# The last two attention iterations of a fused decoder layer as a program of their own

## The chip, the core and the metric
The kernel runs on one core of one Trainium2 chip. The metric is the device time of one execution in microseconds (us). Engines: TensorE (PE; its weight loads are PEld), VectorE (DVE), ScalarE (ACT), GpSimd (POOL), and SyncE (SP), which issues most DMAs.

## What is computed
A decoder layer over x of shape (8, 256, 256): 8 batches, 256 rows, width 256, all fp32.
```python
x = x + attn(layernorm(x))                    # softmax(exp(-|q - k|^2)) @ v, one head
x = x + cross(ctx, layernorm(x), mask)        # 16 heads of width 16, softmax(q k / 4)
x = x + ffn(layernorm(x))                     # 8 experts, best 2 of each row

logits = xs @ Wg                              # xs: 2048 rows
weights, sel = top_k(logits, 2); weights = softmax(weights)
h = relu(xs @ W1[e] + b1[e])                  # width 1024
out = sum over the 2 experts of weights * (h @ W2[e] + b2[e])
```

## The kernel before
**Stages.** Work on a batch is spread over iterations: in iteration n the stages of batch n (first attention's output, cross-attention's keys and queries), n-1 (maxima of the scores), n-2 (exponentials and weighted values) and n-3 (heads, output product, third norm, router) are issued in an interleaved order, which is written out by hand, per engine, in attention_tensor (L745), attention_scalar (L805), attention_vector (L850), attention_gpsimd (L917) and attention_sync (L939). Iterations run from -1 to 9. Iterations 8 and 9 have no new batch: 8 holds the maxima of batch 7, the exponentials of batch 6 and the output of batch 5; 9 holds the exponentials of batch 7 and the output of batch 6. They are called the drain here. The output of batch 7 is made inside the expert stage.

**Scores.** Queries and keys are split into a high and a low part and stacked over 48 partitions (q_stack, k_stack, three buffers each, by batch modulo 3). They are made twice. st_scores (L1382): 8 steps a batch; TensorE opens a pair of PSUM banks with four mask products (mask_product, L1339, the matmuls of L1346), adds the scores (L1376), and VectorE takes the maxima (L1388). st_maxima (L1393) then transposes the maxima (L1401), and SP writes them with four small DMAs into two more rows of q_stack (L1419). st_exps (L1451): again 8 steps; masks (L1346), products with 50 rows, so that the maximum is taken off (L1445), and ScalarE's exponential of 128 x 1024 (L1462). Which pair a step uses is told by scores_pair (L1350) and exps_pair (L1354): from batch 1 on the maxima have pair 1 and the exponentials pair 0; only batch 7's exponentials use both in turn. TensorE is issued both kinds as quad (L737). After every second exponential st_weighted (L1467, matmuls L1480) makes the weighted values of 4 heads; ScalarE copies them out after every fourth.

**Behind them.** st_heads_transposed (L1492, matmuls L1504), st_transpose "hT" (matmuls L1068), st_output (L1520, matmuls L1099), the third norm (VectorE and GpSimd, then L1021), st_router_transpose (L1550, matmuls L1557), st_router (L1566, matmuls L1572), st_best (L1733).

**Routing.** The rows' places in the experts' tiles are worked out with one-hot tables, in two parts: batches 0 to 4 in the drain, 5 to 7 in the expert stage. Part 0: routing_choice (L1744), prefix_product on TensorE (L1689), routing_counts (L1775), first_tiles (L1847), routing_slots (L1903) and four times routing_table (L1933): one-hot rows (L1948), values (L1953) and three products tile_vals (L1956), all on VectorE. TensorE multiplies each (table_product, L1701), b1_transpose (L1713) follows, and routing_index (L1961) makes the lists of rows. GpSimd then starts the gathers (ex_gather, L2144, the copy L2148 and the indirect DMA L2151).

**Expert stage.** experts (L2004) is a pipeline over 39 tiles of 128 rows: gather, transposes (L2177), first product (L2213), relu and split (L2223, L2230, L2233), second product (L2253), bias and weight (L2265, L2267), and an indirect DMA that adds to the output (L2166). W2 of an expert is loaded by SP (load_expert, L1617) and split into two parts in place, the high one by ScalarE (L1652), the low one by VectorE (L1657), 2048 elements wide; the second product of the first three tiles waits for the splits it needs, that of the fourth for all. The loads take the memory of buffers that the attention no longer needs, so SP waits for the last exponentials (t_tile) of batches 5, 6 and 7, for memory_over (L1581) and for the last transposes (p_hT) between them (experts_sync L1589, experts_rest_sync L1601). SP, like each engine, runs its list in order.

The diff's functions, with the line numbers of the profile:

## Time and profile before
| | us |
|---|---|
| median of 3 runs | 640.5 (638.93 to 642.87) |
| the profiled execution, device time | 644.66 |
| its span, first to last instruction | 642.9 |
| TensorE busy | 574.8 (89%) |
| VectorE busy | 360.0 (56%) |
| ScalarE busy | 331.2 (52%) |
| GpSimd busy | 220.1 (34%) |
| iteration 8, iteration 9, first expert tile | from about 278, 317, 358.7 |

Rows come from one profiled execution of the kernel. Busy times of TensorE are from its start to its modelled end; the granted clock is a share of 2.4 GHz, and 0.5 is the lower of its two levels, 1.2 GHz. A chain is followed back from the last instruction; "issue" is time in which an engine waited for nothing that the profile shows.

### The profile page before, as it was taken

The numbers are of one execution on the slowest core, as the hardware profiler recorded it, in microseconds if no ns is written. First come the engines' busy times: TensorE is split into PE (matmuls) and PEld (weight loads), VectorE is DVE, ScalarE is ACT, GpSimd is POOL, SyncE is SP. The second block draws the span as 40 slices with busy tenths as digits, with TensorE's granted clock in tenths as the row PEclk, the third lists the DMA queues.
The fourth block names the chain that finished last, engine by engine and source line by source line (L and its number), as shares of the span: only waits on it lengthen the run. The fifth ranks groups of instructions, "written<-read, shape, count | busy, mean of one in ns | idle before, by whom it ended". The sixth has DMA issues, their size and how long they took to land.

```text
span 642.9 us, 15591 instructions
## 1 busy us (share of the span) xinstructions
PE 574.8 (89%) x5107; PEld 491.4 (76%) x5108; DVE 360.0 (56%) x856; ACT 331.2 (52%) x723; POOL 220.1 (34%) x289
## 2 busy tenths in 40 slices
PE   4677899999999999865877799999999999999992
PEld 3575667787777777543444799999999999999991
DVE  3647776868686867646465867665233232333321
ACT  4532467555656465422343674555655656555560
POOL 6512212213132321000004514543454555555532
PEclk9978999999999999978567799999999999999996
DMA  8594443545445361720065956566667576676732
GB/s 224 134 154 77 52 82 37 93 60 81 70 65 87 54 98 25 111 67 29 9 198 188 316 203 171 167 173 202 201 177 221 176 213 195 191 216 174 224 94 24
DMA packets 56009, 85.71 MB, mean 133 GB/s; under 512 B 6673, under 2 KB 44721, under 8 KB 55953
## 3 DMA queue, kind: packets, MB, share of 16 engines
q1 hardware_dynamic: 46368, 73.59, 45.2%
q0 software_dynamic: 7872, 10.33, 8.5%
q10 hardware_dynamic: 1712, 1.05, 0.6%
q8 instruction: 34, 0.56, 0.4%
q14 instruction: 23, 0.18, 0.1%
HBM read 62.44 MB, written 9.31 MB: 112 GB/s over the span
## 4 chain that ended last, share of the span: by engine, by line
PE 45%; DMA 30%; DVE 7%; issue 7%; ACT 5%; SPq 3%; POOLq 1%; POOL 1%; DVEq 0%; ACTq 0%
DMA out<-y,scatter_now 26%; PE bank L1099 13%; PE pair L1346 5%; PE bank L1480 5%; PE pair L2213 4%; PE pair L1445 4%; PE bank L2253 3%; SPq L1419 3%; PE pair L1376 2%; PE bank L1068 2%; DMA q_stack<-max_lo 2%; DVE row_max L1388 2%; DMA exp_ring<-L_attn_Wo 1%; PE bank L1572 1%; DMA experts_w<-L_ffn_W 1%
## 5 line engine op out<-in xcount | busy, mean ns | idle before, releaser
L2213 PE MATMUL pair<-slots_t,w_now 128*128 128x128 f32 x1248 | 147.4, 277 | 0.0
L2213 PEld LDWEIGHTS pair<-slots_t,w_now 128*128 128x128 f32 x1248 | 144.1, 194 | 0.1
L2223 ACT ACTIVATE hid<-pair,b_tile 128x128 f32<-128x128 f32 x312 | 88.7, 367 | 54.8 <-PE pair L2213 53.3
L2233 DVE TENSOR_TENSOR hid_lo<-hid,hid_hi 128x1024 fp32r<-128x1024 f32 x39 | 47.8, 1225 | 108.0 <-ACT hid_hi L2230 98.3
L2166 POOL DMA_INDIRECT out<-y,scatter_now x39 | 64.7, 1658 | 114.4 <-DMA out<-y,scatter_now 79.9
L1462 ACT ACTIVATE exp_ring<-pair 128x1024 f32<-128x1024 f32 x64 | 65.7, 1028 | 59.6 <-PE pair L1445 58.5
L1388 DVE TENSOR_REDUCE row_max<-pair 128x4 f32<-128x1024 f32 x64 | 78.3, 1223 | 30.0 <-PE pair L1376 30.0
L2253 PE MATMUL bank<-experts_w,hid_hi 128*128 x624 | 82.7, 285 | 0.0
L2253 PEld LDWEIGHTS bank<-experts_w,hid_hi 128*128 128x128 f32 x624 | 75.8, 188 | 0.0
L2230 ACT ACTIVATE hid_hi<-hid 128x512 fp32r<-128x512 f32 x78 | 49.3, 632 | 4.7
L2151 POOL DMA_INDIRECT slots_in<-xn_rows,gather_now x39 | 41.2, 1055 | 25.8 <-POOL gather_now L2148 15.4
L1001 POOL TENSOR_SCALAR rstd<-moments 128x2 f32<-128x2 f32 x24 | 8.1, 340 | 120.1 <-DVE moments L998 120.0
L2148 POOL COPY gather_now<-gather_idx 128x1 uint32 x39 | 42.0, 1077 | 8.2 <-DVE jump L2000 8.2
L2253 PE MATMUL bank<-experts_w,hid_lo 128*128 x312 | 42.9, 279 | 0.0
L1480 PE MATMUL bank<-exp_ring,v_aug 128*32 128x256 f32 x512 | 39.9, 436 | 2.7 <-ACT exp_ring L1462 2.7
L2183 ACT ACTIVATE slots_t<-bank 128x256 f32<-128x256 f32 x39 | 14.9, 383 | 52.3 <-PE bank L2177 52.3
L2253 PEld LDWEIGHTS bank<-experts_w,hid_lo 128*128 128x128 f32 x312 | 39.1, 188 | 0.0
L1445 PEld LDWEIGHTS pair<-q_stack,k_stack 50*128 50x128 f32 x256 | 20.7, 200 | 23.8 <-issue 23.8
L1346 PE MATMUL pair<-mask_k,ident_bf 64*64 64x512 bf16 x128 | 27.2, 422 | 11.9 <-DMA q_stack<-max_lo 6.9
L1445 PE MATMUL pair<-q_stack,k_stack 50*128 50x256 f32 x256 | 34.6, 351 | 0.0
L1081 ACT ACTIVATE tr_hi<-bank 128x512 fp32r<-128x512 f32 x32 | 19.0, 595 | 26.5 <-PE bank L1068 26.5
L1346 PE MATMUL pair<-mask_q,ident_bf 64*64 64x512 bf16 x128 | 26.2, 406 | 6.5 <-DVE row_max L1388 6.2
(287 smaller groups left out, 1078.5 us busy)
## 6 DMA issues: line engine op xcount, KB each, us to landing
w_now<-L_ffn_W SPq DMA_DIRECT2D x39, 1024.0 KB
experts_w<-L_ffn_W SPq DMA_DIRECT2D x8, 1024.0 KB, 6.0
k_stack<-ck_hi SPq DMA_DIRECT2D x32, 128.0 KB, 4.1
q_stack<-cq_hi SPq DMA_DIRECT2D x32, 128.0 KB, 4.3
ctx_in<-ctx SPq DMA_DIRECT2D x8, 256.0 KB, 2.8
k_stack<-ck_lo SPq DMA_DIRECT2D x16, 128.0 KB, 5.3
q_stack<-cq_lo SPq DMA_DIRECT2D x16, 128.0 KB, 5.2
out<-x SPq DMA_DIRECT2D x7, 256.0 KB, 4.7
```

Source lines behind the costliest of these rows:

```text
L1099: mm = eng.matmul(out, a, b, start=start and i == 0, stop=stop and i == len(pairs) - 1, skip_group_check=True)
L1346: eng.matmul(pair[to, c * 512:(c + 1) * 512], core.ident_bf[left, left], part[left, :, :], start=True, stop=False, skip_group_check=True)
L1388: core.e["maxed"].at(eng.tensor_reduce(maxima, pair[:, :].rearrange("p (c t k) -> p c t k", c=KT, t=KT), AX.X, ALU.max))
L1445: mm = eng.matmul(pair[:, c * 512 + kt * S:c * 512 + (kt + 1) * S], k_stack[rows, i, kt * P:(kt + 1) * P], q_stack[rows, i, :], start=Fals ...
L1462: core.e["exp"].at(eng.activation(slots.rearrange("p c t q -> p (c t q)"), pair[:, :], ACT.Exp, scale=HD ** -0.5))
L1480: mm = eng.matmul(ps[32 * q:32 * q + 32, (g % 2) * S:(g % 2 + 1) * S], core.v_aug[b.p][:, kt, head, :], core.exp_ring[:, head % 8, kt, :], ...
L2166: core.rows_out.at(eng.indirect_dma_start(core.out_rows, bass.IndirectOffsetOnAxis(ap=core.scatter_now[b.p][:, :], axis=0), core.y[b.p][:, ...
L2213: mm = eng.matmul(banks[half][:, f * P:(f + 1) * P], core.w1_now[b.p][:, c, start:start + P], core.slots_t[b.p][:, c, :], start=c == 0, st ...
L2223: act = eng.activation(core.hid[:, g, :], banks[half][:, f * P:(f + 1) * P], ACT.Relu, bias=core.b1_tile[b.p][:, g:g + 1])
L2230: core.m["hid_hi"].at(eng.activation(core.hid_hi[b.p][:, part, :], core.hid[:, part, :], ACT.Copy))
L2233: core.m["hid_lo"].at(eng.tensor_tensor(core.hid_lo[b.p][:, :, :], core.hid[:, :, :], core.hid_hi[b.p][:, :, :].bitcast(F32), ALU.subtract))
L2253: mm = eng.matmul(ps[:, 0:D], left[b.p][:, f, :], core.experts_w[:, bass.ds(x * PLACE + (part * FT * D + f * D), D)], start=term == 0 and ...
```

## The change
1. The attention loop ends after iteration 7; the drain becomes a list of its own for each engine (drain_tensor and the others). TensorE makes all eight maxima steps of batch 7 first, then the eight exponentials of batch 6, then those of batch 7, each two steps at a time: open, open, products, products. Both pairs of banks serve the maxima of batch 7 and the exponentials of batches 6 and 7. The output of batch 5 lies among the maxima and the first exponentials, that of batch 6 among those of batch 7.
2. Routing part 0: the three copies behind the prefix product go to ScalarE (prefix_copies). routing_slots becomes routing_rows and routing_weights, and routing_table becomes routing_hot on VectorE and routing_values, which runs on GpSimd in part 0 (on VectorE as before in part 1). local_vals gets a second buffer. first_tiles moves behind the third table, routing_index behind the last low part of the drain. GpSimd's and VectorE's dependent instructions have a counter each (link, settle).
3. SP: load 2 starts at memory_over, not after the exponentials of batch 6; load 3 after those. ScalarE: split 1 comes among batch 7's maxima, splits 2 and 3 at the end. VectorE: split 1 moves from the drain into tile step 0 of the expert stage, the output and variance of batch 7 ahead of it, and everything of batch 7's norm moves from step 1 to step 0.
4. The stacks are placed anew: that of batch 5 alone, then 7, then 6. st_maxima of batch 7 uses bank 2 in place of bank 0.

```diff
             setup(core, eng)
-            for n in range(-1, NB + 2):
+            for n in range(-1, NB):
                 ATTENTION[name](core, eng, Step(n // 2, n % 2))
+            DRAIN[name](core, eng)
...
-    core.local_vals = [sb(f"local_vals{g}", [3, count(g), LOCAL[g]]) for g in range(2)]
+    core.local_vals = [[local_vals[0], sb("local_vals_odd", [3, count(0), LOCAL[0]])], [local_vals[1]]]
...
+def last_maxima(core, at, g):
+
+    for fn in (scores_open, scores_products):
+        for i in (2 * g, 2 * g + 1):
+            at(0, fn, i)
+
+def last_exps(core, at, back, g):
+
+    for fn in (exps_open, exps_products):
+        for i in (2 * g, 2 * g + 1):
+            at(back, fn, i)
+
+def drain_tensor(core, eng):
+    at = drain(core, "tensor", eng)
+    last_maxima(core, at, 0)
+    at(2, st_heads_transposed)
+    last_maxima(core, at, 1)
+    at(2, st_transpose, "hT")
+    last_maxima(core, at, 2)
+    prefix_product(core, eng, 0)
+    last_maxima(core, at, 3)
+    at(2, st_output)
+    at(0, st_maxima)
+    last_exps(core, at, 1, 0)
+    last_exps(core, at, 1, 1)
+    at(1, st_weighted, 0)
+    last_exps(core, at, 1, 2)
+    at(1, st_weighted, 1)
+    last_exps(core, at, 1, 3)
+    at(1, st_weighted, 2)
+    at(2, st_router_transpose)
+    last_exps(core, at, 0, 0)
+    at(1, st_weighted, 3)
+    at(2, st_router)
+    last_exps(core, at, 0, 1)
+    at(1, st_heads_transposed)
+    table_product(core, eng, 0, 0)
+    last_exps(core, at, 0, 2)
+    at(0, st_weighted, 0)
+    table_product(core, eng, 0, 1)
+    at(1, st_transpose, "hT")
+    last_exps(core, at, 0, 3)
+    at(0, st_weighted, 1)
+    at(1, st_output)
+    at(0, st_weighted, 2)
+    table_product(core, eng, 0, 2)
+    at(0, st_weighted, 3)
+    at(1, st_router_transpose)
+    at(1, st_router)
+    at(0, st_heads_transposed)
+    table_product(core, eng, 0, 3)
+    b1_transpose(core, eng)
+    at(0, st_transpose, "hT")
+
+def drain_scalar(core, eng):
+    at = drain(core, "scalar", eng)
+    at(2, st_transpose, "hT")
+    routing_exp(core, eng, 0)
+    prefix_copies(core, "scalar", eng, 0)
+    split_expert(core, "scalar", eng, 1)
+    at(0, st_maxima)
+    for i in range(6):
+        at(1, st_exps, i)
+    at(1, st_weighted, 1)
+    at(1, st_exps, 6)
+    at(1, st_exps, 7)
+    at(2, st_router_transpose)
+    at(0, st_exps, 0)
+    at(0, st_exps, 1)
+    at(1, st_weighted, 3)
+    for i in (2, 3, 4, 5):
+        at(0, st_exps, i)
+    at(1, st_transpose, "hT")
+    at(0, st_weighted, 1)
+    at(0, st_exps, 6)
+    at(0, st_exps, 7)
+    at(0, st_weighted, 3)
+    at(1, st_router_transpose)
+    split_expert(core, "scalar", eng, 2)
+    at(0, st_transpose, "hT")
+    split_expert(core, "scalar", eng, 3)
+
+def drain_vector(core, eng):
+    at = drain(core, "vector", eng)
+    at(0, st_scores, 0)
+    routing_choice(core, "vector", eng, 0)
+    at(0, st_scores, 1)
+    at(2, st_heads_transposed)
+    for i in range(2, 5):
+        at(0, st_scores, i)
+    at(2, st_transpose, "hT")
+    for i in range(5, 8):
+        at(0, st_scores, i)
+    at(0, st_maxima)
+    at(2, st_output)
+    at(2, st_moments, 2)
+    routing_counts(core, "vector", eng, 0)
+    routing_rows(core, "vector", eng, 0)
+    routing_weights(core, "vector", eng, 0)
+    routing_hot(core, "vector", eng, 0, 0)
+    at(2, st_normalise, 2)
+    routing_hot(core, "vector", eng, 0, 1)
+    at(2, st_router)
+    at(2, st_best)
+    at(1, st_heads_transposed)
+    routing_hot(core, "vector", eng, 0, 2)
+    at(1, st_transpose, "hT")
+    first_tiles(core, "vector", eng)
+    at(1, st_output)
+    at(1, st_moments, 2)
+    routing_hot(core, "vector", eng, 0, 3)
+    at(1, st_normalise, 2)
+    at(1, st_router)
+    at(0, st_heads_transposed)
+    at(0, st_transpose, "hT")
+    routing_index(core, "vector", eng, 0)
+    at(1, st_best)
+
+def drain_gpsimd(core, eng):
+    at = drain(core, "gpsimd", eng)
+    routing_numbers(core, "gpsimd", eng)
+    at(2, st_moments, 2)
+    for c in range(3):
+        routing_values(core, "gpsimd", eng, 0, c)
+    at(1, st_moments, 2)
+    routing_values(core, "gpsimd", eng, 0, 3)
+
+def drain_sync(core, eng):
+    at = drain(core, "sync", eng)
+    core.e["t_tile"].wait(eng, LAST_BATCH.back(2))
+    load_expert(core, eng, 1)
+    memory_over(core, eng)
+    load_expert(core, eng, 2)
+    at(0, st_maxima)
+    at(2, st_output)
+    at(2, st_normalise, 2)
+    experts_sync(core, eng)
+    core.e["t_tile"].wait(eng, LAST_BATCH.back(1))
+    load_expert(core, eng, 3)
+    eng.wait_ge(core.r["order"], 1)
+    eng.wait_ge(core.E["residual_early"], 16 * EARLY_BATCHES)
+    ex_load(core, "sync", eng, Step(0, 0))
+    at(1, st_output)
+    core.e["t_tile"].wait(eng, LAST_BATCH)
+    load_expert(core, eng, 7)
+    at(1, st_normalise, 2)
+    eng.wait_ge(core.r["table"], 4)
+    ex_load(core, "sync", eng, Step(0, 1))
+    core.e["p_hT"].wait(eng, LAST_BATCH)
+    load_expert(core, eng, 4)
+    for b in range(2):
+        core.rows_in.wait(eng, Step(0, b))
+    for x in (5, 6):
+        load_expert(core, eng, x)
+
...
 def scores_pair(core, b, i):
-    return core.pair[1 if b.v > 0 else i % 2]
+    return core.pair[i % 2 if b.v in (0, NB - 1) else 1]
 
 def exps_pair(core, b, i):
-    return core.pair[0 if b.v < NB - 1 else i % 2]
+    return core.pair[i % 2 if b.v >= NB - 2 else 0]
 
 def scores_open(core, name, eng, b, it, i):
     if i == 0:
         core.q_stacked.wait(eng, b)
         core.k_stacked.wait(eng, b)
-    if b.v == 0:
-        core.e["maxed"].wait(eng, b if i >= 2 else b.back(1), i - 2)
+    if b.v in (0, NB - 1):
+        if i >= 2:
+            core.e["maxed"].wait(eng, b, i - 2)
+        elif b.v > 0 and i == 0:
+            core.e["exp"].wait(eng, b.back(2))
+        elif b.v > 0:
+            core.e["maxed"].wait(eng, b.back(1))
     elif i == 0:
         core.e["maxed"].wait(eng, b.back(1))
     else:
...
 def st_maxima(core, name, eng, b, it):
-    ps = core.psum[0]
+    ps = core.psum[0 if b.v < NB - 1 else 2]
     if name == "tensor":
-        bank_free(eng, b, (core.e["ksq"], -2, 0), (core.e["cq_split"], -1, 1))
-        if b.v == NB - 1:
-            eng.wait_ge(core.r["counted"], 1)
+        bank_free(eng, b, (core.e["ksq"], -2, 0), (core.e["cq_split"], -1, 1), (core.e["hT_lo"], 2, 0))
         core.e["maxed"].wait(eng, b)
         for qt in range(KT):
             mm = eng.transpose(ps[0:H, qt * P:(qt + 1) * P], core.row_max[:, qt, :], core.ident[:, :])
...
-    if b.v == NB - 1 and i >= 2:
+    if b.v >= NB - 2 and i >= 2:
         core.e["exp"].wait(eng, b, i - 2)
-    elif b.v == NB - 1 and i == 1:
-        core.e["maxed"].wait(eng, b)
+    elif b.v == NB - 2:
+        core.e["maxed"].wait(eng, b.back(-1), 6 + i)
+    elif b.v == NB - 1:
+        core.e["exp"].wait(eng, b.back(1), 6 + i)
     elif i >= 1:
...
-        ps = core.psum[qt if b.v < NB - 1 else qt + 1]
+        ps = core.psum[qt if b.v < NB - 2 else qt + 1]
         if name == "tensor":
-            if b.v == NB - 1:
+            if b.v >= NB - 2:
                 core.e[("x2", "gate")[qt]].wait(eng, b.back(1))
...
+def prefix_copies(core, name, e, g):
+
+    r, n = core.r, PARTS[g].stop - PARTS[g].start
+    within, totals = (ap.rearrange("p (t e) -> p t e", e=NE) for ap in prefix_banks(core, g))
+    e.wait_ge(r["prefix"], g + 1)
+    for dst, src in ((core.totals, totals), (core.running[0], totals), (core.within, within)):
+        if name == "scalar":
+            e.activation(dst[:, 0:n, :], src, ACT.Copy).then_inc(r["counted"], 1)
+        else:
+            e.tensor_copy(dst[:, 0:n, :], src).then_inc(r["counted"], 1)
...
+def routing_hot(core, name, e, g, c):
 
     r, j, n, width = core.r, c // 2, count(g), LOCAL[g]
     first = PARTS[g].start + c % 2 * n
+    tiles, buf, bufs = slice(first, first + n), c % 2 if g == 0 else 0, 2 - g
+    row_hot, hot, vals = core.row_hot[g][buf], core.local_hot[g], core.local_vals[g][buf]
     if c >= 1:
+        e.wait_ge(r["hot"], 3 * (4 * g + c))
+    if c >= bufs:
+        e.wait_ge(r["slots"], 3 * (4 * g + c + 1 - bufs))
+        e.wait_ge(r["table"], 4 * g + c + 1 - bufs)
+    link(core, name, e.tensor_tensor(hot[:, :, :], bc(core.iota_f[:, 0:width], [P, n, width], 1),
+                                     bc(core.slot_tile[:, j, tiles], [P, n, width], 2), ALU.is_equal))
+    link(core, name, e.tensor_tensor(row_hot[:, :, :], bc(core.iota_f[:, :], [P, n, P], 1),
+                                     bc(core.slot_row[:, j, tiles], [P, n, P], 2), ALU.is_equal))
+    settle(core, name, e)
     for a, val in enumerate((core.token_f[:, tiles], core.weight_hi[:, j, tiles].bitcast(F32),
                              core.weight_lo[:, j, tiles])):
-        link(core, e.tensor_tensor(vals[:, a, :, :], hot[:, :, :], bc(val, [P, n, width], 2), ALU.mult))
-    settle(core, e)
+        e.tensor_tensor(vals[:, a, :, :], hot[:, :, :], bc(val, [P, n, width], 2), ALU.mult).then_inc(r["hot"], 1)
+
+def routing_values(core, name, e, g, c):
+
+    r, j, n, width = core.r, c // 2, count(g), LOCAL[g]
+    first = PARTS[g].start + c % 2 * n
+    tiles, buf, bufs = slice(first, first + n), c % 2 if g == 0 else 0, 2 - g
+    tile_vals, vals = core.tile_vals[g][buf], core.local_vals[g][buf]
+    e.wait_ge(r["hot"], 3 * (4 * g + c + 1))
+    if c >= bufs:
+        e.wait_ge(r["table"], 4 * g + c + 1 - bufs)
     for a in range(3):
-        last = e.tensor_tensor(tile_vals[:, :, a, :, :], bc(core.onehot[:, j, tiles, :], [P, n, NE, width], 3),
-                               bc(vals[:, a, :, :], [P, n, NE, width], 2), ALU.mult)
-    last.then_inc(r["slots"], 1)
-
-
...
-            for b in range(4):
+            for b in range(2):
+                ex_gather(core, name, eng, Step(b // 2, b % 2))
+            st_moments(core, name, eng, LAST_BATCH, it, 2)
+            for b in range(2, 4):
                 ex_gather(core, name, eng, Step(b // 2, b % 2))
         elif n in (2, 3):
             at(-2, ex_gather)
         elif n is None or n >= 6:
             at(0, ex_gather)
-        if n == 1:
-            st_moments(core, name, eng, LAST_BATCH, it, 2)
...
             split_expert(core, name, eng, 2)
         elif n == 1:
-            st_output(core, name, eng, LAST_BATCH, it)
-            st_moments(core, name, eng, LAST_BATCH, it, 2)
             split_expert(core, name, eng, 3)
-            st_normalise(core, name, eng, LAST_BATCH, it, 2)
             split_expert(core, name, eng, 7)
```

## Rows read from the trace of the kernel before
**Rows 1.** The page, part 2: granted TensorE clock in 40 slices of 16.07 us.
```profile
PEclk9978999999999999978567799999999999999996
```

**Rows 2.** Windows: stretch, length, busy us of PE, PEld, DVE, ACT, POOL; clock, DMA, GB/s.
```profile
278.00:317.00 39.00, 28.25 (x226) 16.22 (x226) 19.13 (x60) 10.21 (x13) 0.94 (x2) 0.67 0.13 41
317.00:355.00 38.00, 27.50 (x199) 16.80 (x197) 23.26 (x82) 14.70 (x16) 7.85 (x10) 0.68 0.56 179
355.00:383.00 28.00, 24.60 (x181) 23.53 (x180) 21.16 (x34) 21.73 (x42) 8.96 (x8) 0.86 0.79 255
...
500.00:600.00 100.00, 100.00 (x881) 100.00 (x880) 32.73 (x60) 58.68 (x168) 54.73 (x61) 1.00 0.67 197
```

**Rows 3.** The chain that ended last: start, us, what; where a DMA stands in it.
```profile
276.16 1.92 DMA q_stack<-max_lo
...
320.51 5.50 DMA experts_w<-L_ffn_W
```

**Rows 4.** The page, part 5: the two big readers of the score banks.
```profile
L1462 ACT ACTIVATE exp_ring<-pair 128x1024 f32<-128x1024 f32 x64 | 65.7, 1028 | 59.6 <-PE pair L1445 58.5
L1388 DVE TENSOR_REDUCE row_max<-pair 128x4 f32<-128x1024 f32 x64 | 78.3, 1223 | 30.0 <-PE pair L1376 30.0
```

**Rows 5.** The chain at the full clock: one double step, then weighted values.
```profile
253.44 0.56 PE pair L1346 x8
253.99 0.44 PE pair L1445 x4
254.43 0.24 PE pair L1376 x4
254.67 1.00 PE bank L1480 x16
```

**Rows 6.** The chain: the same at half clock, a hand-over, last exponential, last output product.
```profile
306.21 1.00 PE pair L1346 x5
307.21 0.73 PE pair L1445 x4
307.93 0.43 PE pair L1376 x4
308.36 1.86 PE bank L1480 x16
...
328.91 0.64 PE pair L1346 x4
329.55 0.73 PE pair L1445 x4
...
347.92 1.03 ACT exp_ring L1462
...
355.96 2.91 PE bank L1099 x12
```

**Rows 7.** Busy time of three short stretches, columns as in rows 2.
```profile
297.60:303.40 5.80, 0.03 (x4) 0.03 (x4) 5.32 (x31) 0.28 (x1) 0.00 (x0) 0.85 0.00 1
303.40:311.00 7.60, 7.60 (x52) 4.39 (x53) 3.01 (x4) 2.64 (x3) 0.00 (x0) 0.50 0.10 35
333.00:339.00 6.00, 6.00 (x61) 4.09 (x61) 5.75 (x19) 2.65 (x3) 1.18 (x2) 1.00 0.13 45
```

**Rows 8.** GpSimd's groups by shape, 120 to 270 us.
```profile
L1641 POOL TENSOR_TENSOR experts_w<-experts_w 128x256 fp32r<-128x256 f32 x8 | 5.9, 734 | 0.0
L1314 POOL TENSOR_TENSOR x<-x,bias_xattn_bo 128x512 f32<-128x512 f32 x4 | 5.2, 1295 | 21.2 <-DVE x L1308 21.2
```

**Rows 9.** The timeline, 320 to 368 us: start, us, engine, line, operation.
```profile
321.93 1.55 DVE L1956 TENSOR_TENSOR tile_vals<-onehot,local_vals 128x400 fp32r<-128x400 f32 x3
...
347.62 1.98 POOL L2148 COPY gather_now<-gather_idx 128x1 uint32 x1 [8.20 <-DVE jump L2000]
...
358.66 0.63 PE L2177 MATMUL bank<-ident,slots_in 128*128 128x128 f32 x2
```

**Rows 10.** The gathers' tile slots_in over the span: DMA time.
```profile
DMA to landing us min/median/max: 4.1/4.4/4.6
```

447 lines of the change are left out of this document (191 added, 256 removed).

## The prediction
> **What bounds the kernel now.** I read the windows by stage first, then the page's clock line, then the chain. From 500 to 600 us TensorE is busy for 100.00 of 100.00 us at the full clock (2.4 GHz) [rows 2]: the expert stage is bound by TensorE, and whatever is won before it moves its end by as much. The two drain iterations, 278 to 317 and 317 to 355 us, are different: TensorE is busy for 28.25 of 39 and 27.50 of 38 us, at a mean granted clock of 0.67 and 0.68 [rows 2], and these are the slices where the clock line falls to 5 to 8 tenths [rows 1]. So the 77 us hold 28.25 x 0.67 + 27.5 x 0.68 = 37.6 us of work at the full clock. The other 39 us are 21 us of idle time and some 18 us lost to half clock (1.2 GHz).
>
> The chain names the idle time. At 276.16 it stands on the DMA that puts the maxima into the stack, and from 320.51 on a 5.50 us DMA of expert weights [rows 3]: in both iterations the first exponential needs the maxima of the iteration just finished, and the second time ScalarE has an expert split, waiting for its load, ahead of it. From 297.6 to 303.4 TensorE does 0.03 us while VectorE does 31 small instructions (counts and tile tables) for 5.32 us [rows 7] ahead of a maximum. Maxima (1.22 us on VectorE) and exponentials (1.03 us on ScalarE) have one pair of banks each in iteration 8 [rows 4], so each can be made only after the last was read.
>
> **The change, part by part.** The times are those of the profiled execution: span 642.9 us, device time 644.66; the median of the runs is 640.5, 4.2 lower. I carry the difference over to the median.
>
> *Stage A: eight maxima of batch 7 alone.* VectorE sets it: 8 x 1.22 = 9.8 us of maxima [rows 4]. Between them stand the choice, batch 5's heads and its low part. VectorE's 19.13 us between 278 and 317 less 9.8 for maxima and 5.32 for the table block leave 4.0 [rows 2, 7]; about 3.2 of such work falls into stage A (an estimate). Steps now come in twos on two pairs: the opening of the second waits for the maximum just before, so VectorE waits for one mask and one product, 0.64 + 0.73 us at half clock [rows 6] and 0.1 for the signal, 1.5 us. Of four hand-overs the small work hides two. TensorE is too idle here to keep its clock, I assume, as between 303.4 and 311, where it is 0.50 after the hole ahead of it [rows 7]. VectorE can begin at about 276.2, as the chain leaves iteration 7 [rows 3]: 276.2 + 9.8 + 3.2 + 3.0 = 292.2. Batch 5's output product (2.91 us at half clock [rows 6]) lies beside the last two maxima but for about 1.0; the transposes of the maxima take 0.6 and the first exponential's mask and product 1.7. First exponential: 295.5 (now about 279). The DMA of the maxima is now hidden behind eight exponentials of batch 6.
>
> *Stage B: sixteen exponentials.* A group is two exponentials and one batch of weighted values. ScalarE needs 2 x 1.03 us [rows 4], and a hand-over stands between two groups (the second opening's masks and the signal 0.46, most of the 0.56 for two; a product 0.44 [rows 5]; together 0.90): 2.96 us at the full clock. TensorE needs 0.56 + 0.44 + 0.24 + 1.00 = 2.24 of these [rows 5]. At half clock it needs 1.00 + 0.73 + 0.43 + 1.86 = 4.02 [rows 6] and is itself the bound. The rest of TensorE's work is 37.6 - 12 x 1.24 - 8 x 1.00 = 14.7 us; about 3.2 of it lies in stage A, 11.5 in B.
> Full clock: 295.5 + 8 x 2.96 = 319.2; the rest fits mostly into the 0.7 us that each group leaves and beside ScalarE's copies, and I add 2 us for the router of batch 5, which waits for ScalarE. From the last exponential (start 347.92) to the end of the last transposes, 0.75 ahead of the output product at 355.96 [rows 6], it takes now 7.3 us with the exponential; I take 8 from its end, because batch 6's router stands in the queue too. End of the drain: 329.2 (now 355.2).
> Half clock: 295.5 + 8 x 4.02 + 2 x 11.5 = 350.7, and 3 for the last waits: 353.7.
> I take the full clock for three quarters: in B TensorE has 8 x 2.24 + 11.5 = 29.4 us of work for 34 us, 87%, and from 333 to 339, where it had work throughout, the clock was 1.00 [rows 7]; but the stretch 303.4 to 311 was as busy and stayed at 0.50 [rows 7], so B can begin low. 329.2 + 24.5 / 4 = 335.3.
>
> *Routing on GpSimd.* The three tile_vals products of each table, 1.55 us on VectorE [rows 9], go to GpSimd, 12 instructions of 400 elements. GpSimd takes 734 ns for 256 elements and 1295 for 512 [rows 8], so 1.05 us for 400 on that line: 3.1 a table. The trace has none with such broadcast patterns; bounds are 0.52 us (VectorE's) and 2.9 (each held up once like the copy of one column at 347.62, which took 1.98 us [rows 9], some 1.8 of them waiting). I take 1.05, nearest to rows 8; at 2.9 the last table would come 1.7 us too late (rival 3's sum). The tables begin when VectorE is through with maxima, output and counts, near 300, and are wanted by TensorE from 310 on, one per 3 to 6 us: hidden. VectorE loses 6.2 us of work, and the table block no longer stands ahead of a maximum; TensorE's 5.8 us hole goes.
>
> The Trainium skill (GPSIMD Engine Reference, section 8, Key points) says that GpSimd shares its SBUF interfaces with VectorE and contends with instructions that have two SBUF inputs. The trace agrees in one place: a 1-column copy took 1.98 us on GpSimd at 347.62 [rows 9]. By that rule the 12 products would be stretched by what VectorE does beside them, which is the upper bound above.
>
> *What is late next.* Now the index table is ready 8 us ahead of the last transposes and the gather is hidden. In the new order the index follows the last low part on VectorE. From the end of the transposes: 1.4 for high and low part, 1.2 for the index, 0.8 for GpSimd's copy and issue, 4.4 for the gather [rows 10] = 7.8 us to the first expert tile, against 358.66 - 355.2 = 3.5 now [rows 9]. That costs 4.3. First tile: 335.3 + 7.8 = 343.1.
>
> *Expert splits and loads.* ScalarE's splits 1 to 3 lie in waits of the drain; one VectorE split (2.3 us) moves behind the drain, beside which TensorE has the first hidden products and now idles for some 3.4 of 28 us [rows 2]: 0, with 2.3 as the other end. Loads of weights 4 to 6 still start from the last transposes and the first gathers, so they move with them. SP waits for the tile order (about 317) before it stores batch 6's output; nobody waits for that. Nothing after the first tile changes: TensorE is full, the end follows.
>
> Sum: 358.66 - 343.1 = 15.6 us. 644.66 - 15.6 = 629.1 in the profiled execution's terms, 640.5 - 15.6 = 624.9, said as 625, for the median.
>
> **The rivals.**
> 1. *The clock comes back early in B and stays:* drain ends at 329.2, first tile 337.0, gain 21.7: 619. For it: the output product of batch 5 is dense work right ahead of B. Against: hand-overs in every group.
> 2. *The clock stays at half:* drain ends at 353.7, first tile 361.5, 2.8 us later than now, less what a denser order loses less in the first expert tiles: 643, no change. For it: 303.4 to 311, 0.50 through 7.6 busy us [rows 7]. Against: 333 to 339. The Trainium skill (TensorE: Matmul & The Clock Gate, section "A second HAM failure mode: psum-queue depth-cycling") reports a kernel in which small idles between groups of matmuls, made by cycling through PSUM banks, let the clock swing between its levels; two pairs handed to and fro are such cycling. By it this rival would hold.
> 3. *Slower: GpSimd is the bound.* If a product with these patterns takes v us, the tables follow each other at 3v from 300.5, with the variance of batch 6 (1.5 us) in the queue, and what follows the last (table product, index, gather) takes 8: first tile at 310 + 12 v. It decides from 12 v > 33, v > 2.8, and is slower than now from v > 4.05. At v = 4.6, 365: 647. For it: broadcasts over four dimensions and contention [rows 9]. Against: the line of rows 8, a quarter of that.
> 4. *The gain is lost again in the first expert tiles*, because splits and loads are the bound there (ScalarE busy for 21.73 of 28 us [rows 2]): half of it stays, 633.
>
> **How the numbers follow.** Chances: forecast 0.48, rival 1 0.27, rival 2 0.12, rival 3 0.05, rival 4 0.08. About 1% (6.4 us) is what a measurement of this kernel can tell from no change. Faster by over 1% (below 634.1): forecast, rival 1 and most of rival 4, 0.82; same: 0.13; slower 0.05. The likeliest one's own range is 619 to 632 (share of full clock between a half and all). For 8 in 10 the range reaches below rival 1 (615 less estimates for the waits in B, 612) and into rival 2: 612 to 641.
>
> **What would show it.** Windows over the drain: first exponential of batch 6 near 295, eight maxima from 276 to 292; the last transposes near 335; no wait for the maxima's DMA ahead of an exponential; the PEclk line with fewer low slices. TensorE idle for some 4 us ahead of the first expert tile (L2177's counterpart near 343), released by the gather. GpSimd's products at about 1.05 us each. Wrong would be: exponentials paced at 4 us per group (clock), TensorE waiting for GpSimd at a table product, or the second expert tile waiting for splits. If the first tile comes 15 us earlier and the end does not, TensorE was not the bound after 400 us.

## The result, and the profile after

The changed kernel took 625.6 us (median of 4 runs, 621.4 to 626.0) against 640.2 us (4 runs, 638.9 to 642.9) beside it: ratio 0.974, 95% interval 0.971 to 0.977. A second time, together with the experiments, it was 626.5 against 640.9, ratio 0.975 (0.970 to 0.980). The forecast was 625. By the medians the gain is 14.5 us; the ratio, whose interval reaches just to the quotient of the two medians (0.977), puts it at some 16.5. The profiled executions have spans of 642.9 and 624.3 us, 18.6 apart; the one of before lay some 4 us above its median, as the prediction said, and the changed one lies on its own.

The clock line of the changed kernel's page, and from its list of groups the two of [rows 4]:
```profile
PEclk9969899999999999996996899999999999999997
L1512 DVE TENSOR_REDUCE row_max<-pair 128x4 f32<-128x1024 f32 x64 | 78.0, 1222 | 22.9 <-PE pair L1500 22.9
L1586 ACT ACTIVATE exp_ring<-pair 128x1024 f32<-128x1024 f32 x64 | 65.0, 1028 | 30.4 <-PE pair L1569 27.1 <-PE bank L1604 2.3
```
A maximum and an exponential take what they took. Over the whole span, ScalarE's idle time ahead of exponentials fell from 59.6 us to 30.4, and in place of a row of low slices [rows 1] stand two short dips with 9 between them.

Windows, columns as in [rows 2]: maxima, clock coming back, the exponentials, end of the drain, the wait for the gather, first expert tiles:
```profile
276.00:292.00 16.00, 11.92 (x82) 8.12 (x78) 12.00 (x18) 2.99 (x6) 1.33 (x7) 0.69 0.43 133
292.00:300.00 8.00, 6.61 (x66) 3.15 (x64) 6.63 (x35) 4.28 (x6) 0.94 (x2) 0.78 0.13 39
300.00:320.00 20.00, 19.03 (x228) 11.83 (x225) 12.29 (x51) 14.05 (x17) 7.78 (x9) 1.00 0.41 122
320.00:333.00 13.00, 8.29 (x51) 6.58 (x50) 5.92 (x17) 3.49 (x5) 4.23 (x5) 0.74 0.59 204
333.00:341.00 8.00, 3.59 (x14) 2.93 (x14) 5.99 (x18) 2.03 (x3) 4.88 (x7) 0.71 0.87 292
341.00:354.00 13.00, 10.94 (x74) 10.73 (x74) 11.09 (x10) 10.01 (x21) 11.77 (x9) 0.78 0.87 272
```
From 300 to 320 us TensorE is busy for 19.03 of 20 us at the full clock, where before it had 0.67 and 0.68 over the two iterations of the drain [rows 2]. Behind it come two waits, each with a lower clock.

The timeline, VectorE, ScalarE and TensorE (start, us, engine, line, operation, wait before it and who ended it):
```profile
276.01 1.23 DVE L1512 TENSOR_REDUCE row_max<-pair 128x4 f32<-128x1024 f32 x1 [0.31 <-PE pair L1500]
...
284.30 1.23 DVE L1512 TENSOR_REDUCE row_max<-pair 128x4 f32<-128x1024 f32 x1 [1.46 <-PE pair L1500]
...
288.71 2.36 DVE L1512 TENSOR_REDUCE row_max<-pair 128x4 f32<-128x1024 f32 x2 [1.46 <-PE pair L1500]
293.37 1.94 ACT L1586 ACTIVATE exp_ring<-pair 128x1024 f32<-128x1024 f32 x2 [0.62 <-PE pair L1569]
296.61 1.94 ACT L1586 ACTIVATE exp_ring<-pair 128x1024 f32<-128x1024 f32 x2 [1.30 <-PE pair L1569]
299.96 1.94 ACT L1586 ACTIVATE exp_ring<-pair 128x1024 f32<-128x1024 f32 x2 [1.42 <-PE pair L1569]
302.84 1.94 ACT L1586 ACTIVATE exp_ring<-pair 128x1024 f32<-128x1024 f32 x2 [0.45 <-PE pair L1569]
305.72 1.94 ACT L1586 ACTIVATE exp_ring<-pair 128x1024 f32<-128x1024 f32 x2 [0.45 <-PE pair L1569]
308.94 1.94 ACT L1586 ACTIVATE exp_ring<-pair 128x1024 f32<-128x1024 f32 x2 [0.78 <-PE pair L1569]
313.14 1.94 ACT L1586 ACTIVATE exp_ring<-pair 128x1024 f32<-128x1024 f32 x2 [2.27 <-PE bank L1604]
317.28 0.60 ACT L1612 ACTIVATE heads_t<-bank 128x512 f32<-128x512 f32 x1 [1.71 <-PE bank L1604]
317.78 1.94 ACT L1586 ACTIVATE exp_ring<-pair 128x1024 f32<-128x1024 f32 x2
325.08 0.63 PE L1684 MATMUL bank<-ident,xn_ffn 128*128 128x128 f32 x4 [3.48 <-DVE xn_ffn L1140]
331.35 1.11 PE L1187 MATMUL bank<-ident,heads 128*128 128x128 f32 x4
340.14 0.69 PE L2319 MATMUL bank<-ident,slots_in 128*128 128x128 f32 x2 [4.00 <-DMA slots_in<-xn_rows,gather_now]
341.85 6.09 PE L2355 MATMUL pair<-slots_t,w_now 128*128 128x128 f32 x32
```
A row with x2 holds two instructions, one behind the other. Eight maxima stand between 276.0 and 291.1 with two visible hand-overs. The first exponential comes at 293.4 and the last ends at 319.7. The eight groups of two follow each other at 3.2, 3.4, 2.9, 2.9, 3.2, 4.2 and 4.6 us, 3.5 on average. Then TensorE waits 3.48 us for the normalised rows of batch 6, and 4.00 us for the gather. The first expert tile is at 340.1, against 358.66 [rows 9]: 18.5 us earlier, as much as the spans differ.

### The profile page after: what moved, and what is told of

Read it like the earlier page. It is cut to its first block, busy times and chain, and to the rows that moved or that the text cites. A ratio compares the mean times of both kernels' runs of the same rounds, so it can differ in the third digit from the quotient of the medians.

```text
span 624.3 us, 15593 instructions
## 1 busy us (share of the span) xinstructions
PE 565.2 (91%) x5107; PEld 489.0 (78%) x5108; DVE 357.6 (57%) x841; ACT 331.2 (53%) x726; POOL 232.7 (37%) x301
## 3 DMA queue, kind: packets, MB, share of 16 engines
q10 hardware_dynamic: 1712, 1.05, 0.6%
## 4 chain that ended last, share of the span: by engine, by line
PE 77%; DVE 7%; ACT 4%; DMA 4%; issue 4%; SPq 2%; POOL 1%; ACTq 0%; POOLq 0%; DVEq 0%
PE pair L2355 22%; PE bank L2395 17%; PE bank L1218 14%; PE pair L1465 5%; PE bank L1604 4%; PE pair L1569 4%; PE pair L1500 2%; PE bank L1187 2%; SPq L1541 2%; DVE row_max L1512 2%; DMA q_stack<-max_lo 2%; PE bank L2319 1%; PE bank L1699 1%; ACT exp_ring L1586 1%; DMA full<-mask_1x1xSxS_ik 1%
## 5 line engine op out<-in xcount | busy, mean ns | idle before, releaser
L1586 ACT ACTIVATE exp_ring<-pair 128x1024 f32<-128x1024 f32 x64 | 65.0, 1028 | 30.4 <-PE pair L1569 27.1
L2293 POOL DMA_INDIRECT slots_in<-xn_rows,gather_now x39 | 42.9, 1099 | 25.9 <-POOL gather_now L2290 15.5
L1604 PE MATMUL bank<-exp_ring,v_aug 128*32 128x256 f32 x512 | 35.1, 393 | 0.9 <-ACT exp_ring L1586 0.9
L1569 PEld LDWEIGHTS pair<-q_stack,k_stack 50*128 50x128 f32 x256 | 19.0, 189 | 20.0 <-issue 20.0
L1465 PE MATMUL pair<-mask_k,ident_bf 64*64 64x512 bf16 x128 | 25.2, 401 | 6.8 <-DMA q_stack<-max_lo 4.1
L1569 PE MATMUL pair<-q_stack,k_stack 50*128 50x256 f32 x256 | 30.6, 328 | 0.0
```

The source lines that it names most:

```text
L1465: eng.matmul(pair[to, c * 512:(c + 1) * 512], core.ident_bf[left, left], part[left, :, :], start=True, stop=False, skip_group_check=True)
L1569: mm = eng.matmul(pair[:, c * 512 + kt * S:c * 512 + (kt + 1) * S], k_stack[rows, i, kt * P:(kt + 1) * P], q_stack[rows, i, :], start=Fals ...
L1586: core.e["exp"].at(eng.activation(slots.rearrange("p c t q -> p (c t q)"), pair[:, :], ACT.Exp, scale=HD ** -0.5))
L1604: mm = eng.matmul(ps[32 * q:32 * q + 32, (g % 2) * S:(g % 2 + 1) * S], core.v_aug[b.p][:, kt, head, :], core.exp_ring[:, head % 8, kt, :], ...
```

## The experiments

All times are medians beside the kernel before on the same chip. "Tile n" is the n-th gather's transposes in the trace, counted from 0. A start read from a trace is that of one profiled execution.

**1 to 3. How much did the two visible faults of the old order hold?** On the kernel before, the counts and tile tables were moved behind the last maximum; the ScalarE split of expert 2 was moved out of the way of an exponential; and both together.
```
-    if choosing:
-        routing_counts(core, eng, 0)
-        first_tiles(core, eng)
...
     at(-1, st_project, "q")
     at(-1, st_value)
+    if choosing:
+        counts_copied(core, eng)
     at(1, st_maxima)
+    if choosing:
+        routing_counts(core, eng, 0)
+        first_tiles(core, eng)
```
```
     elif choosing:
         split_expert(core, "scalar", eng, 1)
-        split_expert(core, "scalar", eng, 2)
     elif placing:
+        split_expert(core, "scalar", eng, 2)
         split_expert(core, "scalar", eng, 3)
```


> The kernel before with one edit: the block of counts and first tile tables (31 small VectorE instructions, 5.3 us) moved from ahead of maximum 4 of batch 7 to behind the last maximum; the three copies stay ahead of the maxima's transposes. Theory A (the gain of 14.5 us is the new order as a whole: hidden maxima DMA, two pairs, dense work): this hole alone is worth at most 5 us, since the block then stands ahead of batch 6's heads; ratio to before 0.992 to 0.998. Theory B (the gain is mostly two stalls, this one and ScalarE's wait for a weight load): 6 us or more, ratio below 0.991.

> The kernel before with ScalarE's split of expert 2 moved from the end of iteration 8 to the end of iteration 9, so that batch 7's first exponential no longer stands behind a wait for a 1 MB load. It starts at about 323 in place of 327.85. Theory A: 2 to 4 us (the maxima's DMA, to 321.7, is still waited for), ratio 0.993 to 0.997. Theory B: 5 us and more, ratio below 0.992.

> The kernel before with both edits (counts behind the last maximum, split of expert 2 late). Theory A: 5 to 8 us together, ratio 0.988 to 0.992, about half of the change's gain; the rest needs the order. Theory B: 12 us and more, ratio at or below 0.981, with no new order at all.

Measured: counts late 636.6 us, ratio 0.992 (0.990 to 0.995), tile 0 at 350.1 instead of 358.66. Split late 641.7, ratio 0.999 (0.997 to 1.002). Both 634.3, ratio 0.990 (0.987 to 0.993), tile 0 at 349.7. With the split alone moved, the exponential that had stood behind the load [rows 3] waited for something else; the timeline of that run:
```profile
324.59 1.02 ACT L1462 ACTIVATE exp_ring<-pair 128x1024 f32<-128x1024 f32 x1 [3.61 <-PE pair L1445]
```
It comes some 3 us earlier, and waits for scores. The expected 2 to 4 us aren't there in the times, and no more can be said from the traces. Counted from the last exponential ahead of the drain (270.04, 269.16, 271.72 and 268.55 us in the four executions), tile 0 comes after 88.6 us before, and after 81.0, 85.5 and 81.1 in the three runs; in the changed kernel it is 69.1 (from 271.03). By that count the gains would be 7.6, 3.2, 7.5 and 19.5 us, where the medians show 5.1, 0, 7.4 and 14.5. The one trace of before was 4 us above its median, and part of that probably lies in the drain.

By the medians the table block was worth 5.1 us and both 7.4 of the change's 14.5, by the ratios 5.0 and 6.4 of 16.5: four to five tenths of the gain could be had without a new order. The rest came with the new order as a whole. That is theory A of the expectations. The drain of before, of run 3 and of the changed kernel, up to the end of batch 7's transposes, columns as above (run 3's starts as long ahead of its first maximum as that of before):
```profile
276.20:355.20 79.00, 56.59 (x427) 33.44 (x427) 43.66 (x146) 24.90 (x28) 10.47 (x19) 0.68 0.34 108
273.80:346.20 72.40, 51.90 (x425) 31.10 (x423) 43.00 (x145) 23.22 (x27) 10.29 (x18) 0.72 0.37 119
276.00:332.50 56.50, 45.85 (x419) 29.68 (x415) 36.85 (x119) 24.32 (x31) 14.28 (x23) 0.82 0.42 133
```
Worked out as in the prediction (busy time times clock is work at the full clock), these are estimates of 22.4, 20.5 and 10.7 us in which TensorE idles, and of 18, 15 and 8 us lost to half clock. The new order took some 10 us of idle time that the two edits left, and with it almost half of the loss by the clock.

**4. Did sharing with GpSimd help?** The changed kernel with its 12 tile_vals products back on VectorE.
```
     routing_hot(core, "vector", eng, 0, 0)
+    routing_values(core, "vector", eng, 0, 0)
```
(the same for the other three tables, and the GpSimd calls taken out)

> The changed kernel with the twelve table products of part 0 back on VectorE (1.55 us a table in place of 2.6 on GpSimd), all else as changed. Theory A (sharing with GpSimd carries little; the order does): within 0.3% of the changed kernel (625.6), 0 to 2 us slower, by the one table that stands ahead of batch 6's norm. Theory C (the share of GpSimd is a large part of the gain): 4 us or more slower, 630 or above.

> The changed kernel again, unedited, as the reference for the runs beside it: 625.6, ratio 0.974 to before.

626.0 us, ratio 0.976 (0.973 to 0.979), beside 0.975 (0.970 to 0.980) for the changed kernel: the sharing carries nothing that can be measured. (The new order was kept; only the engine of the products changed.) Where a product stood beside VectorE's normalisation, that took 1.83 us; without it 0.73. The timelines of the changed kernel and of this run:
```profile
323.04 2.62 POOL L2094 TENSOR_TENSOR tile_vals<-onehot,local_vals_odd 128x400 fp32r<-128x400 f32 x3
323.11 1.83 DVE L1140 TENSOR_SCALAR xn_ffn<-x,moments,rstd 128x256 f32<-128x256 f32 x2 [0.48 <-POOL rstd L1122]
```
```profile
320.99 1.55 DVE L2095 TENSOR_TENSOR tile_vals<-onehot,local_vals_odd 128x400 fp32r<-128x400 f32 x3
322.45 0.73 DVE L1141 TENSOR_SCALAR xn_ffn<-x,moments,rstd 128x256 f32<-128x256 f32 x2
323.33 1.09 PE L1685 MATMUL bank<-ident,xn_ffn 128*128 128x128 f32 x4 [3.40 <-DVE xn_ffn L1141]
```
TensorE waits 3.40 us instead of 3.48: the 1.1 us that the normalisation is shorter, VectorE spends on the products ahead of it.

**5. The exposed gather.** The changed kernel with the last table and its index ahead of batch 6's router on both engines.
```
     at(1, st_router_transpose)
+    table_product(core, eng, 0, 3)
+    b1_transpose(core, eng)
     at(1, st_router)
     at(0, st_heads_transposed)
-    table_product(core, eng, 0, 3)
-    b1_transpose(core, eng)
```
(on VectorE, routing_index ahead of at(1, st_router))

> The changed kernel with the fourth table product and the transposes of b1 ahead of batch 6's router, and the index on VectorE ahead of the router's logits, so that the gather starts some 6 us earlier. Theory D (the exposed gather costs its 4.0 us of waiting and also the clock: the first hidden products take 6.1 us at half clock in place of 3.7): 5 to 7 us faster than the changed kernel, 619 to 621. Theory E (the next wait takes its place: splits, loads or the third gather): 0 to 2 us.

625.8 us, ratio 0.976 (0.973 to 0.980): no gain, though the wait is gone. The timeline:
```profile
336.61 0.63 PE L2319 MATMUL bank<-ident,slots_in 128*128 128x128 f32 x2
338.06 3.74 PE L2355 MATMUL pair<-slots_t,w_now 128*128 128x128 f32 x32
338.46 2.27 DVE L1766 TENSOR_TENSOR experts_w<-experts_w 128x2048 fp32r<-128x2048 f32 x1
338.64 2.18 POOL L1120 TENSOR_SCALAR rstd<-moments 128x2 f32<-128x2 f32 x1 [6.13 <-DVE moments L1117]
342.06 1.08 POOL L2293 DMA_INDIRECT slots_in<-xn_rows,gather_now  x1 [0.28 <-POOL gather_now L2290]
344.72 1.14 ACT L2365 ACTIVATE hid<-pair,b_tile 128x128 f32<-128x128 f32 x4 [4.99 <-DVE b_tile L2341]
348.10 0.69 PE L2319 MATMUL bank<-ident,slots_in 128*128 128x128 f32 x2 [4.91 <-DMA slots_in<-xn_rows,gather_now]
```
Tile 0 is 3.5 us earlier and its hidden products take 3.74 us instead of 6.09, at the full clock. But the third gather is issued only at 342.06, behind the last batch's rstd, which took 2.18 us on GpSimd beside VectorE's split of expert 1; and the bias copy stands behind two such splits. TensorE waits 4.91 us at tile 2. That is where most of the won time goes: from tile 0 to tile 4 it is 28.2 us instead of 25.3.

**6 and 7. The pairs.** Maxima one step at a time, and exponentials one at a time, with the rest of the new order kept.
```
-    for fn in (scores_open, scores_products):
-        for i in (2 * g, 2 * g + 1):
+    for i in (2 * g, 2 * g + 1):
+        for fn in (scores_open, scores_products):
             at(0, fn, i)
```
(run 7: the same in last_exps, with this loop as in the changed kernel)

> The changed kernel with the maxima of batch 7 one step at a time (open, products, open, products) on the same two pairs. If the hand-over between twos is real (VectorE waits 1.46 us twice), stage A ends 2.5 to 3 us earlier and the kernel is 2 to 3 us faster than the changed one. If TensorE's masks and products, no longer overlapped, cost more than the hand-over: no change or slower.

> The changed kernel with the exponentials one step at a time. ScalarE waits 0.45 to 1.4 us between groups; single steps remove that but TensorE pays about 0.36 us more a group (0.8 us a step in place of 1.24 for two). Where ScalarE is the bound: 1 to 3 us faster. Where TensorE is (groups with router, heads or tables): the same or up to 3 us slower. I expect within 1.5 us of the changed kernel.

626.3 us, ratio 0.976 (0.972 to 0.980), and 625.3, ratio 0.975 (0.972 to 0.979). With the maxima one at a time their hand-over waits shrink from 1.46 us twice to 0.16 and 0.72, and the eight take 13.4 us instead of 15.1. But from the first maximum to the first exponential it is 16.9 us, where the changed kernel has 17.4 and its repeat 16.8: TensorE's output product of batch 5 and the transposes of the maxima now take the time. Opening in twos isn't what the gain rests on.

No run keeps the new order and gives up the second pair, so what the pairs are worth is not shown. They aren't all of it. Batch 7's eight exponentials had both pairs in turn before the change too, and still they got shorter, before and after:
```profile
327.85:348.95 21.10, 17.04 (x141) 10.48 (x141) 11.18 (x30) 9.75 (x12) 2.93 (x3) 0.81 0.44 141
305.72:319.72 14.00, 13.49 (x158) 8.82 (x154) 7.07 (x40) 9.23 (x11) 4.46 (x6) 1.00 0.51 153
```
TensorE's work in them is the same (13.8 and 13.5 us at the full clock, an estimate as above); its idle time went from 4.1 to 0.5 us, and its clock from 0.81 to 1.00.

**8 to 11. Taking the next waits away one after the other.** Each run adds to the one before, beginning from experiment 5. First, all four gathers ahead of the last batch's moments on GpSimd. Then VectorE's split of expert 1 in the drain and that of expert 2 behind the first bias copy. Then (in run 10 alone) first_tiles ahead of the low transposes of batch 6. And, on run 9, the splits of experts 7 and 5 behind what they held up.
```
-            for b in range(2):
-                ex_gather(core, name, eng, Step(b // 2, b % 2))
-            st_moments(core, name, eng, LAST_BATCH, it, 2)
-            for b in range(2, 4):
+            for b in range(4):
                 ex_gather(core, name, eng, Step(b // 2, b % 2))
+            st_moments(core, name, eng, LAST_BATCH, it, 2)
```
```
     at(0, st_heads_transposed)
+    split_expert(core, "vector", eng, 1)
     at(0, st_transpose, "hT")
...
             st_moments(core, name, eng, LAST_BATCH, it, 2)
-            split_expert(core, name, eng, 1)
             st_normalise(core, name, eng, LAST_BATCH, it, 2)
-            split_expert(core, name, eng, 2)
         elif n == 1:
+            split_expert(core, name, eng, 2)
             split_expert(core, name, eng, 3)
```
```
+    first_tiles(core, "vector", eng)
     at(1, st_transpose, "hT")
-    first_tiles(core, "vector", eng)
```
```
             split_expert(core, name, eng, 3)
-            split_expert(core, name, eng, 7)
...
         at(2, ex_hidden)
+        if n == 2:
+            split_expert(core, name, eng, 7)
         if n == 3:
-            split_expert(core, name, eng, 5)
             st_router(core, name, eng, LAST_BATCH, it)
             st_best(core, name, eng, LAST_BATCH, it)
             routing_choice(core, name, eng, 1)
+            split_expert(core, name, eng, 5)
```


> The kernel of the early index, with one edit: GpSimd issues all four first gathers before the last batch's rstd (it issued two, then the rstd that VectorE's split of expert 1 holds, then the other two). Theory E (the gain of the early index was given back at the third tile): the third tile's transposes leave 348.1 for about 343.5, hidden(1) follows at once, ex_out(0) comes at 349 to 350.5 instead of 354.2, and the kernel takes 621.5 to 623.5 us against 625.8, ratio to before about 0.971. Rival F (from the first tile on TensorE is bound by its own work and by the expert splits further back, so that anything won here is waited away again before the tiles of the long run): third tile earlier, but 625 to 626 us, ratio 0.976.

> As the run before, and VectorE's split of expert 1 stands in the drain, in the wait ahead of the last batch's low transposes, and its split of expert 2 behind the first tile's bias copy. Theory E: the bias copy is there by 338.5 instead of 344.5, ScalarE's first hidden(0) row follows TensorE at about 340 instead of 344.7, GpSimd's rstd of the last batch takes 0.9 us instead of 2.2, ex_out(0) comes at 346 to 348, and the kernel takes 618.5 to 621.5 us, ratio about 0.967. Rival F: ex_out(0) earlier, but the time stays at 624 to 626. Rival G (the split delays output(7) in the drain by its 2.3 us): first tile at 338 to 339 instead of 336.6, and half of the gain gone.

> As the run before, and VectorE does the first tiles' table ahead of the low transposes of hT(6), so that output(6) and its moments don't stand behind it. VectorE idles 3.17 us there and the table takes 3.4 us. Theory H (the VectorE chain, not the exponentials, ends the drain): the idle 3.5 us of TensorE ahead of the last router transposes shrink to about 0.5, the last batch's transposes come 2.5 to 3 us earlier, first tile at about 334, time 2 to 3 us below the run before. Rival (the drain is followed by waits of the same length): less than 1 us.

> The kernel with the splits placed, with two more edits on VectorE: the split of expert 7 stands behind the first tile's hid_lo and no longer ahead of the second tile's bias copy, and the split of expert 5 stands behind the last batch's routing choice and no longer ahead of its router copy. In the run before TensorE waited 3.49 us at the second prefix product for `both`, which VectorE made only at 355.3 behind the split of expert 5 (351.6 to 353.9). Theory E (one wait after the other is uncovered, and each is worth what TensorE then no longer waits): both at about 351, the prefix products follow hidden(2) with less than 1 us of wait, the second tile's hid starts near 345 instead of 346.3, the tile behind them (transposes 360.5) comes near 357, and the kernel takes 3 to 4 us less than the run before: 617.5 to 619.5 us, ratio 0.966 to 0.969. Rival F (the time is set further back): 621 to 623 us, ratio 0.972.

Starts in each profiled execution, read from its timeline; the last three columns are differences of the others (us):
```
run               first exp  tile 0  tile 4  span  | exp..tile 0  tile 0..4  tile 4..end
before                 -     358.66  383.39  642.9 |     -          24.7       259.5
changed             293.37   340.14  365.48  624.3 |    46.8        25.3       258.8
changed, again      294.88   340.98  366.14  625.1 |    46.1        25.2       259.0
5  index early      294.99   336.61  364.76  623.7 |    41.6        28.2       258.9
8  + gathers first  293.59   336.16  364.11  622.9 |    42.6        28.0       258.8
9  + splits placed  290.95   334.07  360.47  619.2 |    43.1        26.4       258.7
10 + tiles early    292.25   334.95  361.33  620.3 |    42.7        26.4       259.0
11 9, splits behind 292.09   335.30  357.78  618.7 |    43.2        22.5       260.9
```
Measured: 624.2 us, ratio 0.975 (0.971 to 0.979); 622.0, 0.973 (0.969 to 0.976); 622.8, 0.973 (0.971 to 0.976); 620.5, 0.9685 (0.966 to 0.971). Up to the first exponential these kernels are all alike, and still the executions differ by up to 4 us there, so the differences of columns are what to compare. From the first exponential to the end it is 330.9 and 330.2 us in the two executions of the changed kernel, and 328.7, 329.3, 328.3, 328.0 and 326.6 in the runs 5 and 8 to 11. Run 8 shows the next wait behind the one removed:
```profile
343.83 0.41 PE L2317 MATMUL bank<-ident,slots_in 128*128 128x128 f32 x2 [1.10 <-issue]
344.07 3.74 PE L2353 MATMUL pair<-slots_t,w_now 128*128 128x128 f32 x32
347.69 1.90 ACT L1761 ACTIVATE experts_w<-experts_w 128x2048 fp32r<-128x2048 f32 x1
349.49 0.58 ACT L1690 ACTIVATE xf_t<-bank 128x512 f32<-128x512 f32 x1
350.12 1.65 PE L1699 MATMUL bank<-gate_w,xf_t 128*128 128x8 f32 x8 [2.31 <-ACT xf_t L1690]
351.63 3.76 PE L2393 MATMUL bank<-experts_w,hid_hi 128*128 x16
```
Tile 2 comes at 343.8 as expected, and then TensorE waits 2.31 us for xf_t, which stands on ScalarE behind the hidden rows that waited for their bias and behind a split of its own; 16 products that take 2.12 us at the full clock then take 3.76. Expected were 621.5 to 623.5 us and the first output products (ex_out(0), L2393) at 349 to 350.5; these came at 351.6, and the time of 624.2 isn't told apart from experiment 5. Run 9 takes that wait away. Its output products start at 345.2, in an execution 2.6 us ahead of run 8's by the first exponential, so about as expected; but its 622.0 us lie just above the expected 618.5 to 621.5: another wait, of 3.49 us, stands a tile further on. Run 11 takes this one:
```profile
345.16 2.14 PE L2393 MATMUL bank<-experts_w,hid_hi 128*128 x16
...
355.53 0.65 PE L1807 MATMUL bank<-both,strict 128*128 128x48 f32 x2 [3.49 <-DVE both L1871]
```
```profile
350.85 3.84 PE L2354 MATMUL pair<-slots_t,w_now 128*128 128x128 f32 x32 [1.17 <-DMA w_now<-L_ffn_W]
354.52 0.32 PE L1807 MATMUL bank<-both,strict 128*128 128x48 f32 x2
...
366.99 5.30 PE L2354 MATMUL pair<-slots_t,w_now 128*128 128x128 f32 x32
```
In run 11 the stretch from tile 0 to 4 is 22.5 us instead of 26.4, and about 2 of these are lost again: the hidden products at 366.99 took 5.30 us, where the others of the series have 3.74. Its ratio of 0.9685 (0.966 to 0.971) is the lowest of all; its interval just parts from that of the changed kernel's first comparison (0.971 to 0.977) and overlaps that of its second (0.970 to 0.980). It is probably some 4 to 5 us faster than the changed kernel (4 by the traces and the ratios, 5 to 6 by the medians), but of the 3 to 4 us expected over run 9 the medians show 1.5. Between two neighbouring runs of the series the times tell nothing apart, and only the traces do. Run 10 missed what was expected (2.5 to 3 us): TensorE's wait ahead of the router transposes went from 3.50 to 2.79 us, since the output, the moments, GpSimd's two rstd steps and the normalisation take the time themselves.

## Why the prediction was right

It said 625 with a range of 612 to 641; 625.6 was measured. The mechanism was the one forecast: less idle time and more of the full clock in the drain, and an end that follows the first tile. That the number fell so close is in part luck, since several of its terms are off and offset each other. By its own steps:

*Stage A* was right and slightly long: first exponential 293.4 for 295.5. Two hand-overs of 1.46 us were seen for two of 1.5. Experiment 6 showed that they don't decide: without most of them the stage is no shorter, since TensorE's output product and transposes fill the time.

*Stage B* did not keep the pace: 3.5 us a group for 2.96. Only the third and fourth intervals have 2.9. The first two still lie partly at the lower clock (3.2 and 3.4; 2.9 each in the repeat, at the full clock), and in the last two (4.2 and 4.6) ScalarE waits 2.27 us ahead of an exponential and 1.71 ahead of a copy, both for TensorE's weighted values. The prediction had 11.5 us of other work for TensorE in this stage, and each group leaves it 0.7 us, 5.8 in eight; that it "fits mostly" there and beside ScalarE's copies was the weak step. Its 2 us for batch 5's router stood in for it: 23.7 + 2 = 25.7 forecast, 26.4 measured (25.5 in the repeat). The clock was nearer to rival 1's than to the three quarters chosen: 0.86 from the first exponential to 305.7, 1.00 from there to the last, and 1.00 throughout in the repeat. The half-clock rival is out for this stage. The Trainium skill (TensorE: Matmul & The Clock Gate, "A second HAM failure mode: psum-queue depth-cycling") spoke for it. Here two pairs handed to and fro at 19.03 busy of 20 us kept 1.00, so for this stage the trace doesn't bear the page's case out.

*The end of the drain* came out between two sums, by errors that offset each other. The forecast was 335.3, rival 1's sum 329.2, measured 332.5. Against rival 1's sum, stage B begins 2.1 us early and is 0.7 long. The term that was mis-sized is the 8 us from the last exponential's end to the last transposes; it measured 12.7. In the forecast the quarter of half clock, 6.1 us that the stage did not lose, covered this. In the 12.7 us stand 3.48 us in which TensorE waits for xn_ffn, behind the tile tables, the output, the moments and two GpSimd steps on one chain, and then half clock: the router's eight products took 1.88 us, against 1.06 for batch 5's at the full clock.

*What is late next* was right: the gather is exposed, released tile 0 as said, 4.18 us in the chain for 4.4, and 7.7 us from transposes to tile 0 for 7.8. Tile 0: 340.1 for 343.1. The chain, in order of time:
```profile
334.55 0.12 DVE gather_idx L2122
334.69 0.18 DVE jump L2137
...
335.13 0.19 POOL gather_now L2290
...
335.92 4.18 DMA slots_in<-xn_rows,gather_now
```
What it was worth was wrong. The prediction priced it at 4.3 us of the end; experiment 5 removed the wait of 4.0 us and gained nothing that the times can tell (some 2 us by the one trace).

*GpSimd*: 0.9 us a product for 1.05, hidden, far from rival 3's 2.8. The prediction feared that VectorE would hold GpSimd; what the runs show is the other direction, VectorE's normalisation at 1.83 us against 0.73 above. The Trainium skill (GPSIMD Engine Reference, section 8, Key points) names VectorE instructions with two SBUF inputs or in a 2-port perf mode as those that contend. The normalisation has one tensor input, and no trace tells whether it ran in such a mode. By experiment 4 the sharing neither costs nor brings anything that can be measured.

*Splits, 0 with 2.3 as the other end*: in the plain changed kernel this can't be priced alone, since the wait for the gather covers it. In the series, once the gather was gone, run 8 (four gathers ahead of the rstd that this split holds up) took 0.2 us out of the stretch from tile 0 to 4, and run 9 (this split and that of expert 2 moved) 1.6 more. That lies within the prediction's 0 to 2.3. The other 3.9 us (26.4 to 22.5), of which some 2 were lost later, are the splits of experts 7 and 5, which the prediction did not price at all.

*"Nothing after the first tile changes"* held in sum (24.7 and 25.3 us to tile 4, 259.5 and 258.8 from there), but not in its reason. TensorE wasn't simply full there: tile 0's products take 6.09 us after the wait instead of 3.74, tile 2 waits another 1.67 us, and the stretch gives way when what is ahead moves. Rival 4 (gain lost in the first tiles) did not happen to the change itself; it did to each improvement on top of it, up to run 8.

The profiled executions differ by 18.6 us, 3 more than the sum of 15.6, and the medians by 14.5, 1 less. The sum was read from a trace 4 us above its median, and the prediction carried the difference over unchanged. The changed kernel's trace lies on its median, so this did not hold, and it offsets the 3 us that the sum was short: here too the close number is partly luck.

## What to carry to other kernels

Where the last iterations of a pipeline no longer overlap with a next one, write their order out by kind, so that both double buffers serve one reader: here ScalarE's waits for scores halved and TensorE was at its full clock for most of the stage. Which part of the new order does it (the pairs, the maxima's DMA hidden, the denser list) is not shown. Try the single long stalls first: moving one block of small instructions gave a third of the gain with one edit. Before counting a removed wait as gained, list what the engines in the same stretch still queue ahead of the next consumer; here three short things stood one behind another (rstd behind a split, a bias copy behind two splits, a routing choice behind a split), and the stretch shrank only when the second and the third were gone too. Long instructions without a deadline belong behind short ones that somebody waits for.

## What the runs showed of the hardware

- A short GpSimd instruction beside a long VectorE one took longer: rstd of 128x2 took 2.18 us beside the 2.27 us split in experiment 5, and 0.23 us in run 9 with no split beside it; in the changed kernel beside a one-hot row of 0.82 us it took 0.86. The opposite way, a VectorE TENSOR_SCALAR with one tensor input took 0.92 us instead of 0.37 beside GpSimd's table products (1.83 and 0.73 for two).
- Behind waits of a few us, work that was still in front of TensorE ran at the lower clock again and again: after 3.48 us the router product took 1.88 us instead of 1.06, after 4.00 us the hidden products 6.09 instead of 3.74, after 2.31 us the output products 3.76 instead of 2.12. So a wait cost more than it shows. Shorter waits came out either way: behind 0.74 and 1.10 us the hidden products took 5.35 in the kernel before (from 366.57), behind 0.76 and 1.10 us they took 3.74 in run 8 (from 344.07). In run 11 it also fell (0.81 from 366 to 375 us) in a stretch with full TensorE, after one 1.17 us and one 0.36 us wait. Ahead of it stand 16 products of one column (from 364.90, 1.92 us); 11 of the same kind at 374.94 were followed by 1.00 (375 to 385 us). Why it fell there stays open.
